# The softmax denominators of a second attention: turned in 32x32 blocks and inverted over 16 columns

## The reference

```python
logits = jnp.einsum('bhqd,bhkd->bhqk', q, k_ctx) / math.sqrt(dk)
logits = logits + mask[None, None]          # causal
probs = jax.nn.softmax(logits, axis=-1)
out = jnp.einsum('bhqk,bhkd->bhqd', probs, v_ctx)
out = out.transpose(0, 2, 1, 3).reshape(Bx, Tx, D_MODEL)
return out @ c_w.T
```

## Time and profile before

| | |
|---|---|
| time, median of 3 | 1447.96 us (1446.43 to 1453.06) |
| profiled execution | 1444.73 us, span 1443.0 us |
| TensorE busy | 1354.7 us, 94% of the span |
| VectorE busy | 1011.7 us, 70% |
| ScalarE, GpSimd busy | 662.4 us and 698.5 us |
| mean granted TensorE clock | 0.98 of full |

### The profile page before, as it was taken

The page is one execution under the profiler, slowest core; times in us unless marked ns, Lnnn a source line. Parts: engine busy times, 40 slices in busy tenths (PEclk is TensorE's granted clock), DMA queues, the critical chain, the costliest instruction groups (busy, mean ns, idle before and its releaser), DMA issues.

```text
span 1443.0 us, 19466 instructions
## 1 busy us (share of the span) xinstructions
PE 1354.7 (94%) x7182; PEld 919.7 (64%) x7206; DVE 1011.7 (70%) x1991; ACT 662.4 (46%) x1151; POOL 698.5 (48%) x836
## 2 busy tenths in 40 slices
PE   6988999999989899999998998999999999999996
PEld 5874445555445454554454437778888888888885
DVE  5997475765557777777766735487678767886776
ACT  6654232232314544445453574455445555454442
POOL 2676040412213213234233366478678768866863
PEclk9999999999999899999999999999999999999998
DMA  9100210202213111134020411522223232432300
GB/s 335 59 1 1 73 59 15 88 16 81 73 49 104 39 45 50 34 98 124 8 75 1 140 47 43 211 110 88 88 88 146 89 107 98 153 139 88 117 30 29
DMA packets 46270, 116.86 MB, mean 81 GB/s; under 512 B 3420, under 2 KB 4448, under 8 KB 42336
## 3 DMA queue, kind: packets, MB, share of 16 engines
q1 hardware_dynamic: 45104, 114.31, 23.5%
q10 hardware_dynamic: 1072, 1.31, 0.3%
HBM read 92.28 MB, written 23.07 MB: 80 GB/s over the span
## 4 chain that ended last, share of the span: by engine, by line
PE 64%; DVE 24%; ACT 5%; POOL 3%; issue 3%; DMA 1%; SPq 0%; POOLq 0%; DVEq 0%; ACTq 0%
PE PS L1648 62%; DVE cm L622 4%; DVE SM L638 3%; DVE PS L824 3%; DVE SM L634 2%; PE PS L1657 1%; DVE tm L622 1%; ACT EX L1232 1%; DMA rw<-in_L_ffn_w_up 1%; DVE SM L639 1%; DVE hm L631 1%; DVE RD L860 1%; DVE SM L628 1%; DVE hm L622 1%; POOL xA L1463 1%
## 5 line engine op out<-in xcount | busy, mean ns | idle before, releaser
L1232 ACT ACTIVATE EX<-PS 128x512 f32<-128x512 f32 (+3 forms) x384 | 170.3, 494 | 166.9 <-PE PS L1648 165.3
L1463 POOL TENSOR_TENSOR ws_g<-rw,ws_g 128x512 fp32r<-128x512 f32 x64 | 138.7, 2167 | 126.7 <-ACT ws_g L1053 126.7
L1463 POOL TENSOR_TENSOR SM<-SM 128x1 f32<-128x1 f32 x128 | 81.4, 636 | 228.4 <-DVE SM L628 225.6
L1567 POOL TENSOR_SCALAR_AFFINE_SELECT EX<-EX 128x128 f32<-128x128 f32 x256 | 75.4, 304 | 198.2 <-ACT EX L1232 194.5
L1648 PE MATMUL PS<-KG,QG 96*128 96x512 f32 (+3 forms) x384 | 144.6, 396 | 27.9 <-DVE SM L824 16.5
L824 DVE CUSTOM_DVE_ANT_0 PS<-PS,MW 128x128 f32<-128x128 f32 (+3 forms) x256 | 122.2, 499 | 35.2 <-PE PS L1648 34.9
L1648 PE MATMUL PS<-QG,KG 98*128 98x512 f32 (+3 forms) x384 | 136.9, 384 | 3.5 <-ACT EX L1232 2.8
L1432 ACT ACTIVATE ab<-hm 128x512 f32<-128x512 f32 x64 | 40.5, 633 | 203.5 <-DVE hm L622 203.5
L1648 PE MATMUL PS<-ws_d,HH 128*128 128x512 f32 x528 | 125.7, 389 | 0.7 <-DVE HH L622 0.7
L634 DVE TENSOR_REDUCE SM<-PS 128x1 f32<-128x512 f32 x128 | 87.4, 683 | 50.9 <-PE PS L1648 50.5
L1648 PEld LDWEIGHTS PS<-QG,KG 98*128 98x128 f32 x384 | 72.7, 194 | 76.1 <-issue 48.8
(11 more groups left out here) (204 smaller groups left out, 2841.8 us busy)
## 6 DMA issues: line engine op xcount, KB each, us to landing
rw<-in_L_ffn_w_gate SPq DMA_DIRECT2D x16, 1024.0 KB, 5.1
rw<-in_L_ffn_w_up SPq DMA_DIRECT2D x16, 1024.0 KB, 5.1
rw<-in_L_ffn_w_down SPq DMA_DIRECT2D x16, 1024.0 KB, 6.8
QG<-qs SPq DMA_DIRECT2D x48, 256.0 KB, 4.3
raw<-in_L_ffn_w SPq DMA_DIRECT2D x3, 2816.0 KB, 11.7
qs<-stg SPq DMA_DIRECT2D x16, 512.0 KB, 3.5
xA<-xs SPq DMA_DIRECT2D x2, 2048.0 KB, 9.1
ys<-xA SPq DMA_DIRECT2D x4, 1024.0 KB, 5.8
```

The lines of the kernel that those rows point to most:

```text
L1232: e.activation(EX[:, n % 16, 0:W], PS[:, score_bank(n), 0:W], ACT.Exp, scale=ISQ, bias=0.0).then_inc(S["ex"], 1)
L1463: return e.tensor_tensor(out, a, b, op)
L1567: e.affine_select(out=p, in_=p, compare_op=ALU.is_ge, fill=0.0, base=0, pattern=[[1, 128]], channel_multiplier=-1).then_inc(S["sel"], 1)
```

## The change

The drain no longer copies bank 7 but turns it (VectorE's transpose) block by block: in each 32x32 block rows and columns change places. Since 32 rows of a block were equal, all 32 columns of a turned block are equal, and one column of each, 16 in all, holds every denominator. One reciprocal of these 16 columns goes into a new small tile `recip`. A second turn reads `recip` with each column repeated 32 times and writes RD, which then holds the inverse denominators as before. The pair stands in slot 27, or 10, where the first of the four pieces was. GpSimd's multiplication moves from slot 40 to 31, from 18 to 13, and for the last half-group from step 3 to step 0 of `project`.

```diff
+        recip = small(16).rearrange("p (n r) -> p n r", r=1)
...
                 w.wait_ge(S["pvd"], 12 * (x // 2) + (12 if x % 2 else 4))
                 w.wait_ge(S["oo"], x)
-                e.tensor_copy(RD[:, :], PS[:, 7, :]).then_inc(S["de"], 1)
-
-            def over(x, piece):
+                e.transpose(RD[:, :], PS[:, 7, :]).then_inc(S["de"], 1)
+
+            def over(x):
 
                 w.wait_ge(S["de"], x + 1)
-                r = RD[:, 128 * piece:128 * piece + 128]
-                e.reciprocal(r, r).then_inc(S["rd"], 1)
+                blocks = RD[:, :].rearrange("p (n r) -> p n r", r=32)
+                w.wait_ge(S["dvs"], did(e.reciprocal(recip, blocks[:, :, 0:1])))
+                e.transpose(blocks, recip.broadcast_to([128, 16, 32])).then_inc(S["rd"], 1)
...
-                    if n % 48 in (27, 30, 33, 36):
-                        over(2 * (n // 48), n % 48 // 3 - 9)
-                    if n % 48 in (10, 12, 14, 16) and n > 48:
-                        over(2 * (n // 48) - 1, n % 48 // 2 - 5)
+                    if n % 48 == 27:
+                        over(2 * (n // 48))
+                    if n % 48 == 10 and n > 48:
+                        over(2 * (n // 48) - 1)
...
-                if step < 4:
-                    over(15, step)
+                if step == 0:
+                    over(15)
...
-                w.wait_ge(S["rd"], 4 * x + 4)
+                w.wait_ge(S["rd"], x + 1)
...
-                    if n % 48 == 18 and n > 48:
+                    if n % 48 == 13 and n > 48:
                         scale(2 * (n // 48) - 1)
-                    if n % 48 == 40:
+                    if n % 48 == 31:
                         scale(2 * (n // 48))
...
-                if step == 3:
+                if step == 0:
                     scale(15)
```

## The result

The changed kernel takes 1435.66 us (median of 4 runs, 1434.76 to 1436.53), the kernel before 1448.56 (4 runs, 1446.43 to 1453.06): a ratio of 0.9907 with a 95% interval of 0.9882 to 0.9931, 12.9 us faster. 1438 was forecast, with a range of 1431 to 1446. The profiled execution took 1436.53 us (span 1434.8), against 1444.73 (1443.0) before. That pair is 8.2 us apart; the other 4.7 us of the medians are scatter between executions, for the profiled execution of before lies 3.8 us under its median and that of after 0.9 above. In the 17 runs of before beside the first experiments it took from 1445.08 to 1454.34 us.

What follows compares the result with a forecast made beforehand. TensorE was taken as the bound, losing gaps waiting for VectorE. Gaps 7.6 and multiplications 1.3 make 8.9, kept at 80% as 7.1; with 1.0 behind the loop and 2.1 clock, 10.2 off 1447.96 gives 1438 us, range 1431 to 1446.

Steps and rivals of the forecast that it cites:

- What bounds: Second attention: TensorE is the bound, VectorE costs only gaps where TensorE waits; its queue gets 41.5 us shorter.
- The new instructions: Drain and reciprocal pair: a 512-column turn takes the copy's 686 ns, a 16-column reciprocal 247 ns.
- The gaps: Second attention: TensorE gaps behind VectorE runs containing removed reciprocals shrink, 7.6 us over ten runs.
- the six single gaps: TensorE gaps near 499, 526 to 528, 577, 582, 748 and 772 us, each shorter than or within one reciprocal's time.
- the four long ones: Gaps at 556.70, 608.96 and behind reciprocals at 636.6 and 706.5 us: 0.87 us each, 3.5 together.
- The moved multiplications: Rotations of units 9 to 11: GpSimd's multiplication no longer runs beside VectorE's, 1.3 us of long gaps goes.
- Behind the loop: Projection: the last GpSimd multiplication starts at about 868 instead of 877.75 us; 1.0 us, bounds nothing and 1.29.
- The clock: TensorE's granted clock falls less after three long gaps: 2.1 us taken, bounds 0 and 5.3.
- Given back: Rival for the second attention: the shorter VectorE queue yields only 4.6 us, giving 1443; chance 0.24.
- The clock stays up: Rival: all 5.3 us of clock return, gaps close whole and others shrink, 17 us, giving 1431; chance 0.10.
- The slow turn: Rival: turns up to 3.76 us hold bank 7 and the queue, giving 1489; at 1.2 us, 1440; chance 0.06.
- one yield, 14%: Share of VectorE queue time that becomes TensorE gaps: 55.7 us of queue bought 7.6 us of gaps.

Runs made afterwards that it cites:

- `dummy_pieces`: The changed kernel plus 45 reciprocals of 128 columns on a spare tile, unwaited, in the removed pieces' slots: 1450.89 us, 1.0006 of before.
- `turns_only`: The changed kernel with GpSimd's multiplications back in old slots 40 and 18 and step 3: 1435.79 us, 0.9914 of before.
- the spread kernels: Kernels whose first-half row-maximum products in groups 5 to 7 are spread over 16 slots; before so spread 1435.65 us, changed 1422.74 us.
- `before_spread`: The kernel before, all pieces kept, with row-maximum products of groups 5 to 7 spread over slots: 1435.65 us, 0.9911 of before.
- `spread_turns_only`: The changed kernel with maxima of groups 5 to 7 spread and GpSimd's multiplications in their old places: 1418.36 us, 0.9801 of before.
- `turns_twice`: The changed kernel with each of its 32 turns made twice, one behind the other: 1445.87 us, 0.9998 of before.
- `lumped`: The kernel before with its four reciprocal pieces back to back in slot 27 or 10, multiplications in the new slots: 1469.1 us, 1.0131 of before.

## Why the prediction was right, point by point

**What bounds.** Right, and shown: `dummy_pieces` puts back nothing but time in VectorE's queue, and the gain is gone. The 41.5 us of queue were worth 12.9 us by the medians, 31%, where the forecast made all its terms 10.2, 25%. (One old piece was taken at 0.87 us; the two starts in the earlier trace rows lie 0.86 apart, which takes 0.6 us off the queue and nothing off the argument.)

**The new instructions.** The turn takes 711 ns out of PSUM and 712 inside SBUF; the copy's 686 was taken. The Trainium skill ("VectorE: DVE Perf Modes", "The three transpose paths") gives 311 ns for 128 columns of bf16, and by the prediction's estimate from it 512 columns had been 711: the trace agrees, for fp32 too. Only this one size was measured. The small reciprocal takes 247 ns, as computed. The 44 us that were named for VectorE's busy time are the work on RD; the busy time itself fell by 37.9.

**The gaps.** In the profiled pair the sum of this term is right: ten runs with a gain of 7.1 us were named, and the waits for maxima fell by 7.2 over the attention. Place by place it is right for the six single gaps, of whose 4.1 us all but 0.2 went, and less so for the four long ones, which were to give 3.5. TensorE after, in order of time, at the two rotations of the earlier trace rows, 556.70 and 608.96:

```profile
554.47 0.50 PE L1651 MATMUL PS<-KG,QG 96*128 96x512 f32 x1 [0.16 <-DVE SM L635]
...
559.49 0.39 PE L1651 MATMUL PS<-KG,QG 96*128 96x256 f32 x1 [1.37 <-DVE SM L635]
...
603.93 0.99 PE L1651 MATMUL PS<-KG,QG 96*128 96x512 f32 x2 [0.31 <-DVE SM L825]
...
608.81 0.39 PE L1651 MATMUL PS<-KG,QG 96*128 96x256 f32 x1 [0.76 <-DVE SM L635]
```

The gap of 1.61 us became one of 0.16 and one of 1.37 behind the second half of the same rotation, over the 1.1 us that the text set as a limit; that of 1.44 became 0.31 and 0.76. The gap of 1.95 us at 641.48, behind the reciprocal at 636.6, broke into 0.84 and 0.85. Only the fourth gave more than its 0.87: the gaps of before from 710 to 716 us fell from 2.3 to 1.0. The prediction has a reciprocal there (706.5) and also calls the burst at 714 free of them; VectorE has no idle time from 706.45 to 713.56, so they are one run. That the total was met is thus in part luck. And the term is mis-sized for the usual execution. `dummy_pieces` measures the same queue at 14.3 us, twice the 7.1. Two things stand beside that. The profiled execution of before was among its fastest, so its gaps need not be those of a usual one (no trace of a slower one is there, and this stays open). And a gap cost more than its own length: in `dummy_pieces` 5.1 us more of waits came with 4.3 us more of busy time.

**The moved multiplications.** This term of the sum failed: the mechanism is right for the one multiplication of each rotation, the 1.3 us are not there. The rotation's first multiplication no longer has company, but what comes behind it has. VectorE after in order of time, then GpSimd:

```profile
556.02 1.31 DVE L623 TENSOR_TENSOR tm<-pt,SIN 128x512 f32<-128x512 f32 x1
...
601.59 0.68 DVE L623 TENSOR_TENSOR tm4b<-pt,COS 128x512 f32<-128x512 f32 x1
...
605.75 0.99 DVE L623 TENSOR_TENSOR tm4b<-pt,SIN 128x512 f32<-128x512 f32 x1
...
609.46 1.15 DVE L623 TENSOR_TENSOR SM<-SM 128x16 f32<-128x16 f32 x1
```

```profile
555.50 1.28 POOL L1466 TENSOR_TENSOR stg<-tm,stg 128x512 fp32r<-128x512 f32 x1
...
609.31 1.26 POOL L1466 TENSOR_TENSOR stg<-tm4b,stg 128x512 fp32r<-128x512 f32 x1
```

An operation on 16 columns takes 1.15 us beside GpSimd's, and this is the chain that ends in TensorE's longest wait for a statistic, the new 1.0 us among the waits. TensorE after, there and behind it; the second row is eight products at the lower clock, the third (from 560.67) eight of the same shape at the upper:

```profile
610.91 0.38 PE L1833 MATMUL PS<-idf,SM 128*16 128x128 f32 x1 [1.65 <-DVE SM L629]
...
611.78 1.51 PE L1651 MATMUL PS<-EX,VG 128*32 128x384 f32 x8
```

```profile
560.67 0.85 PE L1651 MATMUL PS<-EX,VG 128*32 128x384 f32 x8
```

The prediction warned that the moved multiplication could meet other VectorE work with two inputs. What meets it here is another one: GpSimd's own part of the rotation (into `stg`), which did not move in the program. `turns_only` confirms the balance: nothing.

**Behind the loop.** The start came as forecast, 1.9 us behind the drain. Of 1.0 us the gap gives 0.55, and in the spread kernels the step makes no difference. The bound of nothing was the nearer one.

**The clock.** 2.1 us were taken and none came in the profiled pair: the mean from 475 to 866 us is 0.95 where before had 0.96 and 0.96 to 0.98 was forecast, and in the attention the clock was low for 47.8 us and not for 44.4. The falls moved. Windows of after behind the gaps that end at 608.81 and 610.91, and at a burst of maxima that has no reciprocal in it:

```profile
612.00:618.00 6.00, 6.00 (x25) 2.99 (x17) 2.22 (x9) 2.33 (x4) 0.89 (x3) 0.50 0.48 178
...
774.00:780.00 6.00, 5.39 (x12) 3.23 (x12) 5.70 (x25) 0.00 (x0) 0.00 (x0) 0.52 0.00 0
```

Both are at or near 0.50, the lower of the two levels, 1.2 GHz. The prediction gave its bounds as 0 to 5.3, and the lower one is what came. The profile of `turns_only`, with the same time, has 37.5 us at the lower level, so another execution can gain what this one did not. What takes more of it away is the spreading: 34.1 us in `before_spread`, which keeps every reciprocal, and 23.9 with the turns as well, in `spread_turns_only`.

**The rivals.** *Given back* is refuted by the intervals: 1443 would be 0.9966, above 0.9931. *The clock stays up* named 1431, and its clock did not come. *The slow turn* falls with 711 ns, but its price was wrong by far. The prediction put 19 us of queue in longer turns at 2.1 us (14% of 19 is 2.7; 2.1 is what its 80% leave); `turns_twice` measures 13.2 for 21. The step that failed there is the use of one yield, 14%, for all of VectorE's queue. That yield is near what pieces of 0.47 us cost (16%), and far under the 37% of pieces of 0.87 us, from which it was read, and the 63% of longer turns.

**The sum.** 7.1 + 1.0 + 2.1 = 10.2 against 12.9 by the medians. The total came out near in part by luck, because a gap term that was too small for the usual execution stood beside a clock term that did not show in the profile and a term behind the loop that was half there. What carries the 4.7 us between the profiled pair and the medians is open. The mean clock of whole executions points to a part: it was 0.980 in the profiled execution of before and 0.9785 on average in the 17 beside the first experiments, which by an estimate (0.0015 of 1443) is 2 us. It would take traces of several executions of before.

## What to carry to other kernels

Where one engine may run only a few products ahead of another, look for the longest uninterrupted stretch of work in front of each release and not for the sum of busy time: here the same four pieces, put back to back, cost 19 us more, and 21 us of queue cost 3.3 us in short pieces and 13.2 as longer turns (a part of that may be the bank that the drain holds). Shrink an operation before you split it (16 columns that hold all the values in place of 512), and spread the releases themselves, for here the two gains added up. Where executions of a kernel scatter by 9 us, price a queue by putting a dummy load into it, since one profile shows the gaps of one execution.

## What the runs showed of the hardware

- VectorE turns 512 columns of fp32 in 32x32 blocks in 711 ns out of PSUM and in 712 ns out of an SBUF tile whose 16 columns are each read 32 times: 1.39 ns a column, nearly as much as a copy out of PSUM (686 ns), and no dearer for the repeated operand.
- A reciprocal costs 6.2 ns a column with 128 rows (247 ns for 16, 543 for 64, 943 for 128), over four times the turn's rate.
- VectorE's operation with two inputs in SBUF on 16 columns took 1.15 us while a GpSimd multiplication of 1.26 us ran; the median of its eight in the trace is 177 ns.
- TensorE's products of 128x384 took 0.85 us for eight at 2.4 GHz and 1.51 us for eight at 1.2 GHz, and the time at the lower level in this attention ranged from 23.9 us (`spread_turns_only`) to 64.9 (`lumped`) with the same products.
